# Splitting VectorE's chained steps into single instructions and re-ordering all engines in a fused attention and feed-forward layer

## The reference

```python
qkvz = (x_n @ w_qkvz.T)                    # q, k, v, z for 32 heads of 64
mixed = conv1d_causal(q, k, v, taps=4)     # depthwise, 4 taps along the tokens
g = -exp(A_log) * softplus(a + dt_bias); beta = sigmoid(b)
q = l2norm(q) * 64 ** -0.5; k = l2norm(k)
def step(S, (q, k, v, g, b)):              # 256 steps, S is 64 x 64 per head
    S = S * exp(g)
    delta = (v - k @ S) * b
    S = S + outer(k, delta)
    return S, q @ S
o = rmsnorm(o) * norm_weight * sigmoid(z)
y = x + o @ w_out.T + ffn(x_n)             # ffn: fwht, up and gate, silu, fwht, down
```

## Time and profile before

| | |
|---|---|
| median of 3 runs | 810.78 us (810.19 to 812.11) |
| profiled execution | 807.49 us, its span 805.3 us |
| busy: PE, DVE, ACT, POOL | 734.9, 695.5, 326.6, 279.0 us |
| mean granted clock of TensorE | 0.990 |

### The profile page before, as it was taken

The page is one execution under the profiler, slowest core; times in us unless marked ns, Lnnn a source line. Parts: engine busy times, 40 slices in busy tenths (PEclk is TensorE's granted clock), DMA queues, the critical chain, the costliest instruction groups (busy, mean ns, idle before and its releaser), DMA issues.

```text
span 805.3 us, 26961 instructions
## 1 busy us (share of the span) xinstructions
PE 734.9 (91%) x11562; PEld 481.3 (60%) x11562; DVE 695.5 (86%) x1224; ACT 326.6 (41%) x737; POOL 279.0 (35%) x185
## 2 busy tenths in 40 slices
PE   1699999989999999999999999999999998989986
PEld 1445465656565666656666566666566665656664
DVE  4899998999989999998989988998988889987645
ACT  2255335353434444452624345353534353444110
POOL 3033412434261524343161523234262516234110
PEclk9989999999999999999999999999999999999989
DMA  8123240405041322314141321404123232312201
GB/s 224 60 66 92 66 77 24 96 22 97 31 90 47 74 64 39 90 26 76 51 83 40 67 76 24 105 17 81 41 37 101 29 107 30 74 21 32 42 2 53
DMA packets 140406, 49.79 MB, mean 62 GB/s; under 512 B 118144, under 2 KB 131840, under 8 KB 140160
## 3 DMA queue, kind: packets, MB, share of 16 engines
q1 hardware_dynamic: 139664, 47.93, 26.5%
q10 hardware_dynamic: 624, 0.15, 0.2%
HBM read 40.44 MB, written 7.60 MB: 60 GB/s over the span
## 4 chain that ended last, share of the span: by engine, by line
PE 49%; DVE 34%; issue 7%; ACT 4%; POOL 3%; DMA 1%; SPq 1%; DVEq 0%; ACTq 0%; POOLq 0%
PE bank L716 16%; DVE kq L259 13%; PE bank L807 4%; PE bank L737 4%; PE bank L916 3%; PE bank L836 3%; PE bank L864 3%; PE bank L803 2%; PE bank L805 2%; PE bank L744 2%; PE bank L849 2%; PE bank L767 2%; DVE ATP L309 1%; PE bank L819 1%; PE bank L943 1%
## 5 line engine op out<-in xcount | busy, mean ns | idle before, releaser
L716 PE MATMUL bank<-xnT,wq 128*128 128x512 f32 x512 | 252.9, 619 | 6.4 <-DVE kq L259 6.3
L259 DVE SCALAR_TENSOR_TENSOR kq<-bank,cw,kq 128x510 f32<-128x510 f32 (+2 forms) x288 | 213.6, 745 | 13.1 <-ACT kq L1044 6.2
L716 PEld LDWEIGHTS bank<-xnT,wq 128*128 128x128 f32 x512 | 89.2, 191 | 86.0 <-issue 69.1
L1044 ACT ACTIVATE kq<-bank,cw 128x512 f32<-128x512 f32 x96 | 65.9, 687 | 129.3 <-PE bank L716 126.2
L1232 POOL TENSOR_TENSOR Sd<-St,dec 128x256 f32<-128x256 f32 x32 | 20.8, 649 | 267.2 <-DVE St L383 216.8
L1226 POOL TENSOR_TENSOR kqg<-kq,rows 128x1024 f32<-128x1024 f32 x32 | 77.1, 2425 | 71.5 <-DVE kq L259 36.5
L1236 POOL TENSOR_TENSOR ost<-ost,cst 128x8 f32<-128x8 f32 x32 | 55.0, 1719 | 90.1 <-DVE ost L396 89.3
L916 PE MATMUL bank<-wo,oT 128*128 128x256 f32 x256 | 68.4, 384 | 0.1
L737 PE MATMUL bank<-xh,wguT 128*128 128x512 f32 x128 | 57.9, 595 | 1.6 <-DVE hf L271 1.6
L371 DVE TENSOR_TENSOR X<-UT,bank 128x256 f32<-128x256 f32 (+1 forms) x96 | 43.5, 461 | 16.3 <-PE bank L807 8.0
L916 PEld LDWEIGHTS bank<-wo,oT 128*128 128x128 f32 x256 | 45.8, 190 | 16.7 <-issue 11.6
(11 more groups left out here) (129 smaller groups left out, 1247.9 us busy)
## 6 DMA issues: line engine op xcount, KB each, us to landing
wq<-wqkvz_dram SPq DMA_DIRECT2D x16, 512.0 KB, 3.8
rows<-decay_rows SPq DMA_DIRECT2D x64, 128.0 KB, 3.0
rows<-decay_rows SPq DMA_DIRECT2D x32, 256.0 KB, 4.2
inverse_blocks<-UU SPq DMA_DIRECT2D x32, 128.0 KB
UT<-inverse_blocks SPq DMA_DIRECT2D x128, 32.0 KB, 2.4
wguT<-wgu_dram SPq DMA_DIRECT2D x8, 256.0 KB, 3.3
woraw<-wout_dram SPq DMA_DIRECT2D x16, 128.0 KB, 2.6
base_blocks<-ATP SPq DMA_DIRECT2D x128, 16.0 KB, 1.8
```

The costliest lines, as they stand in the source:

```text
L259: nc.vector.scalar_tensor_tensor(out=y[:, :, t:S], in0=p[:, :, 0:S - t], scalar=cw[:, m, i // 2, 3 - t:4 - t], in1=y[:, :, t:S], op0=ALU.m ...
L716: last = nc.tensor.matmul(ring[i % 2][:], wq[:, q, kc, i // 2, :], xnT[:, kc, (i % 2) * 512:(i % 2) * 512 + 512], start=kc == 0, stop=kc = ...
L1044: nc.scalar.activation(kq[:, i // 2, 2 * (i % 2):2 * (i % 2) + 2, :], split(ring[i % 2][:], 2), ACT.Copy, scale=cw[:, m, i // 2, 3:4]).the ...
```

## The change

DVE's `proj` takes the tap as a further number and issues one instruction per step; `inv` issues one of its 16 instructions per step, and `norm` one of two. The instructions, their operands and their sizes are the same. The wait for the previous link stands in front of each step now, except for links 6, 9 and 11 of `inv`, which do not read what the link before them wrote and have no wait any more. DVE's table grows from 657 to 1089 steps. The tables of all five engines are in a new order; the steps of PE, ACT, POOL and SP are the same ones.

```diff
-                def proj(m, q, i):
+                def proj(m, q, i, t):
                     y = kq[:, i // 2, 2 * (i % 2):2 * (i % 2) + 2, :]
                     p = split(ring[i % 2][:], 2)
-                    dve.wait_ge(tap0_done, m * 6 + i + 1)
...
-                    for t in (1, 2, 3):
-                        if t > 1:
-                            dve.wait_ge(conv_step, m * 18 + 3 * i + t - 1)
-                        nc.vector.scalar_tensor_tensor(out=y[:, :, t:S], in0=p[:, :, 0:S - t], scalar=cw[:, m, i // 2, 3 - t:4 - t],
-                                                       in1=y[:, :, t:S], op0=ALU.mult, op1=ALU.add).then_inc(conv_step, 1)
+                    if t == 1:
+                        dve.wait_ge(tap0_done, m * 6 + i + 1)
...
+                    else:
+                        dve.wait_ge(conv_step, m * 18 + 3 * i + t - 1)
+                    nc.vector.scalar_tensor_tensor(out=y[:, :, t:S], in0=p[:, :, 0:S - t], scalar=cw[:, m, i // 2, 3 - t:4 - t],
+                                                   in1=y[:, :, t:S], op0=ALU.mult, op1=ALU.add).then_inc(conv_step, 1)
...
-                def inv(m, q, i):
-
-                    at = [m * NINV + (0, 5, 12)[i]]
+                def inv(m, q, n):
+
                     U = UU[:, 0]
...
-                    def step(ins):
-                        at[0] += 1
-                        ins.then_inc(inv_step, 1)
-                        if at[0] < ends:
-                            dve.wait_ge(inv_step, at[0])
...
+                    if n == 0:
                         dve.wait_ge(nb_in, (m + 1) * 16)
...
+                    elif n not in (6, 9, 11):
+                        dve.wait_ge(inv_step, m * NINV + n)
...
+                    last.then_inc(inv_step, 1)
...
-                def norm(m, q, t):
-
-                    dve.wait_ge(osq_done, m * 2 + t + 1)
-                    nc.vector.tensor_reduce(ost[:, 0, :], sqo[:], AX.X, ALU.add).then_inc(ms_step, 1)
-                    dve.wait_ge(ms_step, m * 2 + t + 1)
...
+                def norm(m, q, t, n):
+
+                    if n == 0:
+                        dve.wait_ge(osq_done, m * 2 + t + 1)
+                        nc.vector.tensor_reduce(ost[:, 0, :], sqo[:], AX.X, ALU.add).then_inc(ms_step, 1)
+                    else:
+                        dve.wait_ge(ms_step, m * 2 + t + 1)
```

Two lines of the tables, DVE's (the other tables are new in the same way):

```diff
-                     8.hz.3.0 8.hz.3.1 10.proj.0 10.proj.1 8.state.0 9.inv.0 8.ks.1 9.inv.1 8.state.1 10.proj.2 8.ks.2 10.proj.3 8.norm.0
...
+                     14.o.1.0 14.o.1.1 14.o.1.2 14.ff 14.out.0 14.turn.1 14.out.1 14.out.2 14.out.3 15.hz.0.0 15.hz.0.1 15.hz.1.0 15.hz.1.1
```

More of the change, by code:

```diff
@@ L539, in _ @@
[L539 to L554, removed]
@@ new lines, in _ @@
+                     3.inv.10 4.proj.2.3 3.inv.11 2.state.1 4.proj.3.1 3.inv.12 2.ks.2 4.proj.3.2 2.norm.0.0 4.proj.3.3 4.proj.4.1
+                     2.norm.0.1 2.state.2 4.proj.4.2 3.inv.13 4.proj.4.3 2.ks.3 2.gated.0 4.proj.5.1 3.inv.14 2.turn.0 3.inv.15 4.proj.5.2
+                     2.norm.1.0 2.norm.1.1 4.proj.5.3 2.gated.1 2.out.0 2.turn.1 2.out.1 3.vtr.0 4.stats 2.out.2 3.vtr.1 4.gram.0 2.out.3
+                     4.gram.1 4.ff 4.gram.2 4.gram.3 3.hz.1.0 3.hz.1.1 5.e 3.hz.2.0 3.hz.2.1 3.hz.3.0 3.hz.3.1 5.proj.0.1 5.proj.0.2
@@ new lines, in _ @@
+                     4.vtr.0 3.out.2 4.vtr.1 5.gram.0 3.out.3 5.gram.1 5.ff 5.gram.2 5.gram.3 4.hz.1.0 4.hz.1.1 6.e 4.hz.2.0 4.hz.2.1
+                     4.hz.3.0 4.hz.3.1 6.proj.0.1 6.proj.0.2 6.proj.0.3 4.state.0 6.proj.1.1 5.inv.0 4.ks.1 6.proj.1.2 6.proj.1.3 5.inv.1
+                     5.inv.2 5.inv.3 5.inv.4 6.proj.2.1 5.inv.5 6.proj.2.2 6.proj.2.3 4.state.1 5.inv.6 6.proj.3.1 4.ks.2 6.proj.3.2
+                     5.inv.7 4.norm.0.0 5.inv.8 5.inv.9 5.inv.10 4.norm.0.1 6.proj.3.3 5.inv.11 4.state.2 6.proj.4.1 4.ks.3 5.inv.12
@@ new lines, in _ @@
+                     6.inv.4 7.proj.3.2 6.inv.5 6.inv.6 5.ks.2 6.inv.7 7.proj.3.3 6.inv.8 5.norm.0.0 6.inv.9 5.norm.0.1 6.inv.10 6.inv.11
+                     7.proj.4.1 5.state.2 6.inv.12 5.ks.3 5.gated.0 7.proj.4.2 6.inv.13 7.proj.4.3 7.proj.5.1 5.turn.0 7.proj.5.2
+                     5.norm.1.0 5.norm.1.1 7.proj.5.3 6.inv.14 6.inv.15 5.gated.1 5.out.0 5.turn.1 5.out.1 7.stats 5.out.2 7.gram.0
+                     7.gram.1 6.vtr.0 6.vtr.1 5.out.3 7.ff 7.gram.2 7.gram.3 6.hz.1.0 6.hz.1.1 6.hz.2.0 6.hz.2.1 8.e 6.hz.3.0 6.hz.3.1
@@ new lines, in _ @@
+                     7.state.2 9.proj.4.1 8.inv.13 7.ks.3 7.gated.0 9.proj.4.2 9.proj.4.3 9.proj.5.1 7.turn.0 8.inv.14 7.norm.1.0
+                     7.norm.1.1 9.proj.5.2 9.proj.5.3 8.inv.15 7.gated.1 7.out.0 7.turn.1 9.stats 7.out.1 8.vtr.0 8.vtr.1 9.gram.0 7.out.2
+                     9.gram.1 7.out.3 9.ff 9.gram.2 9.gram.3 8.hz.1.0 8.hz.1.1 8.hz.2.0 8.hz.2.1 10.e 8.hz.3.0 8.hz.3.1 10.proj.0.1
+                     10.proj.0.2 10.proj.0.3 10.proj.1.1 10.proj.1.2 8.state.0 10.proj.1.3 9.inv.0 9.inv.1 9.inv.2 9.inv.3 8.ks.1 9.inv.4
@@ new lines, in _ @@
+                     9.inv.5 10.proj.2.1 10.proj.2.2 9.inv.6 9.inv.7 10.proj.2.3 9.inv.8 8.state.1 9.inv.9 10.proj.3.1 9.inv.10 9.inv.11
+                     10.proj.3.2 8.ks.2 9.inv.12 10.proj.3.3 9.inv.13 8.norm.0.0 8.norm.0.1 8.state.2 10.proj.4.1 10.proj.4.2 8.ks.3
+                     8.gated.0 10.proj.4.3 9.inv.14 10.proj.5.1 9.inv.15 8.turn.0 8.norm.1.0 10.proj.5.2 8.norm.1.1 10.proj.5.3 8.gated.1
+                     8.out.0 8.turn.1 10.stats 8.out.1 9.vtr.0 9.vtr.1 10.gram.0 8.out.2 8.out.3 10.gram.1 10.ff 10.gram.2 10.gram.3
@@ new lines, in _ @@
+                     14.proj.2.2 14.proj.2.3 13.inv.12 14.proj.3.1 12.state.0 14.proj.3.2 12.ks.1 14.proj.3.3 13.inv.13 13.inv.14
+                     14.proj.4.1 12.state.1 14.proj.4.2 12.ks.2 14.e 12.norm.0.0 12.norm.0.1 12.state.2 14.proj.4.3 12.ks.3 14.stats
+                     12.gated.0 14.proj.5.1 13.inv.15 14.proj.5.2 14.proj.5.3 12.norm.1.0 12.norm.1.1 12.turn.0 14.gram.0 14.gram.1
+                     12.gated.1 12.out.0 12.turn.1 12.out.1 14.gram.2 12.out.2 12.out.3 14.gram.3 15.proj.0.1 15.proj.0.2 15.proj.0.3
@@ L588, in _ @@
+                     15.out.2 15.out.3""")
                 dve.wait_ge(acc_done, PAIRS * 4)
```

388 lines of the change are left out of this document (213 added, 175 removed).

## The result

The changed kernel took 804.25 us (median of 17 runs, 800.28 to 811.06) against 810.81 us of the kernel before in the same rounds: ratio 0.9925, 95% interval 0.9903 to 0.9948, so by the ratio 6.1 us (4.2 to 7.9) faster; the two medians lie 6.6 apart. The profiled execution has a span of 801.4 us.

What follows compares the result with a forecast made beforehand. PE and DVE were taken to bound the kernel in turn, neither full. Terms -9.4 + 1.5 - 1.0 = -8.9 from the profiled 807.49 us gave 798.6, plus 3.3 to the runs' median: 802 us, range 793 to 814.

Steps and rivals of the forecast that it cites:

- the main term: DVE's chains: 27.5 us of waits taken away, priced at the chain's share 0.34, giving -9.4 us at the end.
- The waits inside DVE's chains: DVE's taps, inverse links and norms: waits on the instruction directly ahead fall from 435 to 172, saving 27.5 us of DVE.
- The chain's share, 0.34: DVE's part of the chain that ended last, taken as price of the 27.5 us saved on DVE: -9.4 us.
- Taps that hold their bank: Conv taps holding a bank longer: 0 if PE has other work before its next write, +14 us at most without.
- The loop of the inverse: Inverse chain and its transfers, pair to pair: stretch costs +1.5 us, up to +9; as slower rival 814 us, chance 0.21.
- PE takes over: Rival, whole span: DVE's 27.5 us become idle time, 811.3 us, no change; chance 0.12 together with the no-cost-waits rule.
- The end: Pair 15's tail, with 14.fo and 15.ff reordered around ks.3 and the norm: -1.0 us, between -2.2 and +1.3.

Runs made afterwards that it cites:

- the run with 60 swaps: Kernel before, with 60 DVE swaps of neighbours behind inverse links and norms and no waits at links 6, 9 and 11; 810.6 us, ratio 0.999.
- The run that took 1.9 us of this away: Against the kernel with the old start and then the new order: inverse links 13 to 15 pulled forward in pairs 5 to 10; 797.33 us, ratio 0.9823 to before.
- waits given back to DVE: Kernel after, same orders; each later tap, link and norm waits for the DVE instruction directly ahead instead of its own predecessor; 823.47 us, ratio 1.016 to before.
- the chains put together: Kernel after, with DVE's taps, links and norms whole again at their last piece's place, other engines' orders as after; 888.37 us, ratio 1.0972 to before.
- that with more waits: Kernel after, same order; later taps, most links and second norms also wait for the DVE instruction directly ahead; 839.13 us, ratio 1.0353 to before.

## Why the prediction was right, and where not

The forecast was 802 us, 8.9 less than before; measured are 6.1 less. The sign held, and the saved waits are seen in the trace. But the price of the main term did not hold, the end's term is not shown, and the start was missing from the sum. That the total came near is in part luck: behind the start the change brought more than the forecast, and the start took half of it back.

- *The waits inside DVE's chains, 0.11 us each.* Right in size: 0.11 to 0.13 us where a wait was taken away, 0.03 to 0.04 us of gap where it was put to the neighbour. The Trainium skill's page "VectorE: DVE Perf Modes", section "The DRAIN you can't avoid", has a semaphore between chained instructions cost nothing; these gaps differ from it, and here the measurement decides. The DVE time saved was 27.5 us by the count; the profile shows 23.5 us less busy time, and busy time can show only the overlap, 0.08 of each 0.11 us, an estimated 20 us.
- *The chain's share, 0.34, as its price.* This step failed. In the old order no price is seen: 12 us of DVE taken away in the run with 60 swaps gave a ratio of 0.999, at most 0.24 of the 12 us by its interval. In the new order it is about 0.6. The share of DVE in the chain tells how often DVE ends a wait, not what happens when it does so earlier. That in the old order PE's next step stood behind something else is the likely reason, but no run shows what. The price of the split and the new order cannot be told apart in the -12.4 us that they brought together from pair 3 on.
- *Taps that hold their bank, 0 with cover, +14 without.* In the old order, where PE's list has no such cover, holding back 76 third taps cost 29 us, twice the prediction's upper end. With PE's new order the wait for the taps fell to 4.3 us, though 115 second and third taps no longer follow the tap before directly. That fits the cover; the new list without it was not run. The forecast had said under 3; 2.8 of the 4.3 us are four projections before 92 us, in the first pairs:

```profile
82.41 1.98 PE L759 MATMUL bank<-xnT,wq 128*128 128x512 f32 x4 [1.18 <-DVE kq L260]
91.69 1.98 PE L759 MATMUL bank<-xnT,wq 128*128 128x512 f32 x4 [0.91 <-DVE kq L260]
```
- *The loop of the inverse, +1.5, at most +9.* It shows, as 3.5 us of PE waiting for X (1.48 of it in the first pairs) and 2.4 us of DVE for UU, 0.6 and nothing before. The run that took 1.9 us of this away put a longer wait for og in its place, and its time differs by -2 us, give or take 4. So the loop is there and small, it did not decide, and its price stays open.
- *PE takes over.* From pair 5 to 9 the change gained nothing, as this rival has it, but not for its reason alone: waits given back to DVE cost 6.6 us in these pairs. Pairs 1 to 5 gained 6.9 us and pairs 9 to 14 another 7.1, which a price for the whole span could not say.
- *The end, -1.0.* From the same product to the last sum 24.6 us, against 798.68 + 1.29 - 773.75 = 26.2 in the profile of before. That the order alone saved it is not shown: by the eleven profiles above the old tail would take about as long as the new one at full clock, and the difference goes with stretches at half clock, which only the old tail has. The prediction had no term for the clock.
- *What was missing altogether: the first pairs.* No term priced the new order of pairs 0 to 2. It costs 6.3 us (ratio 0.9925 against 0.9847; with both intervals 3 to 10). In the trace the first state copies come 3.5 and 5.1 us later, the second with a half clock ahead of it. Which step in these pairs costs it was not tried; PE waits there 1.48 us for the first inverse's transfer into X, 1.1 us for ATP and 1.2 and 0.9 us for taps at the two projections shown above. Before, the same stretch (56 to 130 us) had two larger waits of PE, 1.6 us for hf and 1.5 for yacc.

So the sum in the runs' numbers is: the split and the new order from pair 3 on -12.4, the new start +6.3, together -6.1. The forecast had -8.9 for the first, 0 for the second.

## What to carry to other kernels

Splitting a dependent chain saves the gap and the lost overlap of each link, here 0.11 us, but that has to be met by an order of the other engines that uses the time. In the old order 60 swaps gave nothing, and moving the link that frees a bank by one place, 76 times, cost 29 us. Price a new order by stretches, with the first and last iterations on their own: each may gain or lose several microseconds that a mean over the span hides. When a planner's new order wins in one stretch and loses in another, try the old order for the losing stretch; here that gave another 0.8%.

## What the runs showed of the hardware

The runs of one kernel differ by up to 11 us, and the larger part of it goes with TensorE's mean granted clock: a straight line through the runs has 6.2 us for each 0.01 of clock in the kernel after (17 runs, correlation -0.8) and 6.1 in the kernel before (45 runs beside the experiments, -0.87), with some 1.5 us left over. Every profile has three or more stretches at 1.2 instead of 2.4 GHz, of 3.4, 6.8 or 10.2 us, at different places: near 38 and 775 us and at the end before; near 35, 162 and 513 us and at the end after. What PE did ahead of the one at 513 was to stand still for 0.88 and 1.77 us with short products between. In the recurrence of the last pair before, in which the clock fell at 775 us, it stood still for 0.56 and 0.53 us between short products.

Two kernels that make PE wait more also lost clock: 0.977 with the delayed taps and 0.956 with the chains put together, against 0.987 and 0.988 beside them. At 6.1 us per 0.01 that is an estimated 6 of the former's 29 us and 20 of the latter's 78, which no wait in the list shows. It does not follow for every slower kernel: that with more waits took 839 us at 0.988. The kernel after had a mean clock of 0.9887 over its 17 runs; for the kernel before the groups beside the experiments had 0.9882, 0.9867 and 0.9864. The runs of the kernel before in the result itself have no clock on record, so of the 6.1 us up to 1.5 may be the clock's (an estimate from these means).
